# Attention scores from two float32r parts with two heads in the halves of TensorE's array, in place of three 16-bit parts and one head at a time

## What is computed

```python
Q, K, V = proj(Wq, bq), proj(Wk, bk), proj(Wv, bv)
lam = LAMBDA_MAX * jnp.exp(-ALPHA * u_prev)
use_sparse = lam >= SPARSE_THRESHOLD
scores = einsum('bhqd,bhkd->bhqk', Q, K) * scale
dense_out = softmax(scores + lam * where(prior_mask, 0, -1)) @ V
# where use_sparse: attention over 32 listed keys of each query instead
...
x = x + causal_attention(prior_attention(x))
x = x + moe_ffn(gated_mixer(x))
```

## Time and profile before

| | before |
|---|---|
| runs (us) | 1667.03, 1668.97, 1670.23; median 1668.97 |
| span of the profiled execution | 1660.4 us, first to last instruction |
| outside that span, against the median | 8.6 us |
| busy share: TensorE / weight loads / DVE / ACT / POOL | 94% / 46% / 52% / 44% / 42% |
| attention up to 1022.6 us, tail from there | 1022.6 / 637.8 us |

### The profile page before, as it was taken

One profiled execution on the slowest core, in us unless ns is written; L12 is line 12 of the kernel. 1 busy time (PEld: TensorE's weight loads), 2 busy tenths in 40 slices (PEclk: granted clock), 3 DMA queues, 4 the chain that ended last, 5 costly groups with the idle time before them and its releaser, 6 DMA issues. The chain is left out here.

```text
span 1660.4 us, 20515 instructions
## 1 busy us (share of the span) xinstructions
PE 1558.2 (94%) x7392; PEld 762.5 (46%) x7392; DVE 869.0 (52%) x2041; ACT 734.8 (44%) x998; POOL 696.3 (42%) x515
## 2 busy tenths in 40 slices
PE   5789999989999999899999888999999999999998
PEld 3423333323333333333433334555656577777755
DVE  7578878888678855557765733342422111111141
ACT  4754666766566665476645566223211111111111
POOL 4437999987799998143210120400001200000070
PEclk9559999999999999999998898999999999999999
DMA  3551033243231310344532015100040005243071
GB/s 97 143 155 33 24 80 76 70 98 78 60 85 35 79 46 8 79 117 109 125 73 64 28 33 166 61 0 0 0 152 4 22 1 183 92 162 114 16 129 24
DMA packets 75905, 121.43 MB, mean 73 GB/s; under 512 B 14920, under 2 KB 53265, under 8 KB 72731
## 3 DMA queue, kind: packets, MB, share of 16 engines
q1 hardware_dynamic: 72155, 113.62, 24.3%
q0 software_dynamic: 3072, 6.03, 2.1%
q10 hardware_dynamic: 576, 0.47, 0.1%
HBM read 85.08 MB, written 36.96 MB: 74 GB/s over the span
## 5 line engine op out<-in xcount | busy, mean ns | idle before, releaser
L1141 POOL TENSOR_TENSOR sb_prob<-sb_prob,sb_weight 128x1024 f32<-128x1024 f32 x192 | 448.0, 2357 | 44.6 <-ACT sb_prob L1355 44.1
L1355 ACT ACTIVATE sb_prob<-wide 128x1024 f32<-128x1024 f32 (+3 forms) x384 | 347.5, 916 | 207.9 <-PE wide L1965 109.1
L1960 PE MATMUL wide<-sb_stack_q,sb_stack_k 99*128 99x512 bf16 (+3 forms) x896 | 282.8, 364 | 16.2 <-ACT sb_prob L1355 7.4
L1399 ACT ACTIVATE sb_sil<-wide 128x320 f32<-128x320 f32 (+1 forms) x128 | 66.2, 517 | 436.0 <-PE wide L2039 436.0
L1644 DVE CUSTOM_DVE_ANT_0 sb_junk<-bank,sb_bias 128x512 bf16<-128x512 f32 x339 | 226.8, 688 | 61.7 <-PE bank L1933 57.0
L1933 PE MATMUL bank<-sb_stack_k,sb_stack_q 96*128 96x512 bf16 (+3 forms) x597 | 217.3, 380 | 17.1 <-DVE sb_rowmax L1638 5.8
L2039 PE MATMUL wide<-sb_weight,sb_ffn 128*128 128x512 f32 x512 | 232.3, 597 | 0.0
L1980 PE MATMUL wide<-sb_prob,sb_v_aug 128*17 128x512 f32 (+3 forms) x1792 | 221.2, 560 | 7.6 <-ACT sb_o_raw L1368 6.2
L1638 DVE TENSOR_REDUCE sb_rowmax<-bank 128x1 f32<-128x512 f32 (+3 forms) x258 | 139.2, 559 | 88.3 <-PE bank L1936 57.1
L1771 DVE TENSOR_TENSOR sb_act_s<-sb_sil,wide 128x512 f32<-128x512 f32 x64 | 43.9, 687 | 253.3 <-ACT sb_sil L1399 253.3
L1179 POOL DMA_INDIRECT sb_weight<-slots_out,sb_slot_r x32 | 31.5, 984 | 285.0 <-issue 283.2
(11 more groups left out here) (272 smaller groups left out, 1831.7 us busy)
## 6 DMA issues: line engine op xcount, KB each, us to landing
sb_stack_k<-parts SPq DMA_DIRECT2D x32, 256.0 KB, 6.8
o_raw<-sb_o_raw SPq DMA_DIRECT2D x32, 256.0 KB, 2.3
sb_big<-rg SPq DMA_DIRECT2D x8, 1024.0 KB, 4.9
sb_big<-ru SPq DMA_DIRECT2D x8, 1024.0 KB, 7.3
sb_big<-rd SPq DMA_DIRECT2D x8, 1024.0 KB, 10.7
sb_stack_q<-parts SPq DMA_DIRECT2D x16, 384.0 KB, 4.9
parts<-sb_o_norm SPq DMA_DIRECT2D x40, 128.0 KB
sb_stack_q<-parts SPq DMA_DIRECT2D x16, 256.0 KB, 5.4
```

Source lines behind the costliest of these rows:

```text
L1141: e.tensor_tensor(p, p, weight_of(*u[1:]), ALU.mult).then_inc(weigh_p.handle, 1)
L1355: e.activation(p[:, :, first:HALF], sc[:, :, first:HALF], ACT.Exp).then_inc(SC.empty_sem(u), 1)
L1399: e.activation(sil[:, i % 2, 0:n], SC.tile(u)[:, 0:n], ACT.Silu).then_inc(silu_a.handle, 1)
L1960: i = e.matmul(sc[:, j * HALF + first:(j + 1) * HALF], stack_k[0:ROWS_M, n % 3, g, kt * P:(kt + 1) * P], stack_q[0:ROWS_M, n % 3, g, half ...
```

## The change

- Queries and keys are split in two float32r parts (`hi`, rounded by ScalarE, and the rest by one subtraction on POOL), where three 16-bit parts were. `second`, `middle` and `third` become one step, `split`.
- Three products of parts are kept, not six: `ROWS` is 48, with two rows for the maximum 50. Two heads of a pair lie on partitions 0 to 49 and 64 to 113 of one stack; the stack's two rows of -1 come from one memset of the whole `stack_k` by POOL at the start, in place of three DMAs of ones.
- Score matmuls of a unit stand one behind the other, before the `cut` matmuls. Maxima go in pairs of heads, and the diagonal's mask matmuls stand behind both of a pair. The order of the first plan changes with it: two heads' maxima stand with each table.
- `fin` has three steps (VectorE, ScalarE, POOL); `turn` is two steps of four float32r matmuls of 128 columns each, each with four DMAs; the scores of a half wait for its own.
- A stack takes eight DMAs; DRAM parts are float32.

```diff
-PARTS = 3
-Q_PART = [0, 1, 2, 0, 1, 0]
-K_PART = [0, 1, 0, 1, 0, 2]
+PARTS = 2
+Q_PART = [0, 0, 1]
+K_PART = [0, 1, 0]
+STRIP = P // 2
-FIN_STEPS = 6
-FIN_AT = (0, 1, 1, 3, 3, 5, 6, 7)
-STACK_LOADS, LATER = 7, 4
+FIN_STEPS = 3
+FIN_AT = (0, 1, 1, 2, 3, 3)
+STACK_LOADS, LATER = 8, 4
-SPLIT_FIRST, SPLIT_AT = (1, 1, 1), (1, 4, 5)
+SPLIT_WAIT = 1
...
 def maxima(n):
-    return [("max", n, h, qt, half) for h in range(QUAD) for qt in range(NT) for half in range(NH)
-            if not causal or half * HALF < (qt + 1) * P]
+    return [("max", n, h, qt, half) for pair in range(PAIRS_OF) for qt in range(NT) for half in range(NH)
+            for h in range(PAIRS_OF * pair, PAIRS_OF * (pair + 1)) if not causal or half * HALF < (qt + 1) * P]
...
-        return with_tables(maxima(m)) if JOBS[m] == (0, 1, 0) else maxima(m)
+        return in_pairs(with_tables(maxima(m)) if JOBS[m] == (0, 1, 0) else maxima(m))
...
-        plan += [("turn_count", t), ("kb", 0, t)] + [u for u in steps if u[2:4] == (0, t)]
+        plan += [("turn_count", t), ("kb", 0, t)] + [u for u in steps if u[2] < PAIRS_OF and u[3] == t]
...
-    for k, u in enumerate([u for u in steps if u[2]]):
-        plan.append(u)
-        if k % 4 == 0 and tables:
+    for k, pair in enumerate(in_pairs([u for u in steps if u[2] >= PAIRS_OF])):
+        plan += pair
+        if k % 3 != 2 and tables:
             plan += tables.pop(0)
...
-        parts = dram("parts", [2, B, 2, PARTS, DH, H, S], BF16)
+        parts = dram("parts", [2, B, 2, PARTS, DH, H, S], F32)
...
-        stack_q = s1("stack_q", [P, 3, QUAD, S], BF16)
-        stack_k = s1("stack_k", [P, 3, QUAD, S], BF16)
+        stack_q = s1("stack_q", [P, 3, PAIRS_OF, S])
+        stack_k = s1("stack_k", [P, 3, PAIRS_OF, S])
...
+            e.memset(stack_k[:], -1.0).then_inc(const_done.handle, 1)
...
-                if u[0] == "second":
+                if u[0] == "split":
+                    hi, rest = SPLIT[u[1], u[2]][SET[u[1:]]]
                     w.wait_ge(BK.emptied(("product", *u[1:])))
-                    e.tensor_tensor(val, val, hi, ALU.subtract).then_inc(split_p.handle, 1)
-                elif u[0] == "third":
-                    w.wait_ge(split_a.after(("middle", *u[1:])))
-                    e.tensor_tensor(lo, val, mid, ALU.subtract).then_inc(split_p.handle, 1)
+                    e.tensor_tensor(rest.bitcast(F32R), rest, hi, ALU.subtract).then_inc(split_p.handle, 1)
...
-                    i = e.matmul(bk[:, 0:hi - lo], stack_q[0:ROWS, n % 3, h, qt * P:(qt + 1) * P],
-                                 stack_k[0:ROWS, n % 3, h, lo:hi], start=True, stop=not diag)
-                    if diag:
-                        i = e.matmul(bk[:, hi - lo - P:hi - lo], C["ident"], C["neg_qk"], start=False, stop=True)
-                    i.then_inc(BK.full_sem(u), 1)
+                    pair, j = divmod(h, PAIRS_OF)
+                    rows = slice(j * STRIP, j * STRIP + ROWS)
+                    i = e.matmul(bk[:, 0:hi - lo], stack_q[rows, n % 3, pair, qt * P:(qt + 1) * P].bitcast(F32R),
+                                 stack_k[rows, n % 3, pair, lo:hi].bitcast(F32R), start=True, stop=not diag)
+                    if not diag:
+                        i.then_inc(BK.full_sem(u), 1)
+                    elif j == PAIRS_OF - 1:
+                        for g in range(PAIRS_OF):
+                            v = ("max", n, PAIRS_OF * pair + g, qt, half)
+                            e.matmul(BK.tile(v)[:, hi - lo - P:hi - lo], C["ident"], C["neg_qk"], start=False,
+                                     stop=True).then_inc(BK.full_sem(v), 1)
...
                     for j in range(PAIRS_OF):
-                        g = PAIRS_OF * pair + j
+                        rows = slice(j * STRIP, j * STRIP + ROWS_M)
                         i = e.matmul(sc[:, j * HALF + first:(j + 1) * HALF],
-                                     stack_k[0:ROWS_M, n % 3, g, kt * P:(kt + 1) * P],
-                                     stack_q[0:ROWS_M, n % 3, g, half * HALF + first:(half + 1) * HALF],
+                                     stack_k[rows, n % 3, pair, kt * P:(kt + 1) * P].bitcast(F32R),
+                                     stack_q[rows, n % 3, pair, half * HALF + first:(half + 1) * HALF].bitcast(F32R),
                                      start=True, stop=not to_pool(n, v))
-                        if to_pool(n, v):
+                    if to_pool(n, v):
+                        for j in range(PAIRS_OF):
```

205 lines of the change are left out of this document (96 added, 109 removed).

## The result

The changed kernel takes 1793.97 us (median of four runs, 1788.49 to 1807.75) against 1669.6 us for the kernel before: a ratio of 1.0754, 95% interval 1.0727 to 1.0781. It is slower by 7.5%, outside the range given. The profiled execution has a span of 1806.0 us (the run itself 1807.75), 145.6 more than the 1660.4 before. Its mean granted clock was 0.892, that of the other three 0.898 to 0.904, so the excess probably lies where the clock was low; there is one trace only, so this isn't shown.

A forecast was written before the change was run, and what follows sets the result against it. TensorE, busy 94% of the span, was taken as the bound. Prior jobs -30, causal jobs -9 and start -9 made -48 us: 1621 us against the median of 1669, range 1590 to 1680.

The forecast's parts named there:

- I take 0.22: TensorE, scores and maxima: a float32r pair in two row halves takes 0.22 us, between bounds of 0.22 and 0.86.
- Rival 2: TensorE weight loads: a pair's two float32r loads run one after the other, 0.38 us per pair; 1672 us, chance 0.10.
- Rival 3: TensorE pairs: float32r takes two cycles per column or halves don't overlap, 0.43 us per pair; 1712 us, chance 0.14.
- 680 x 0.10 = 68 us: TensorE, prior and causal jobs: 680 added changes between row halves and other arrangements cost 0.10 us each.
- 113 were forecast: Prior jobs, TensorE: scores and maxima in pairs save 512 x 0.22 = 113 us.
- Rival 1, hand-over in pairs: Three banks of maxima: a pair needs two at once, so VectorE and TensorE wait; +22 us, 1643 us, chance 0.14.
- Together -30 of the 77: Prior jobs: of TensorE's net 77 us, 30 shorten the stage, since other engines, mostly POOL, bound it next.
- Causal: of 13 I take -9: Causal jobs: of TensorE's net 13 us saved, 9 shorten the stage, as 38 us are already idle.
- Before the first score: -9: Start: shorter products' chain, filled VectorE waits and a shorter `fin` bring the first score 9 us sooner; bounds -14 and +3.
- the two terms of 4: Start: products' chain without ScalarE's rounding and a POOL subtraction, -4; four maxima filling VectorE's waits, less the hand-over, -4.
- The first score waits for as many DMAs as before: nothing: Start: second `turn` and its DMAs come behind the first half's, so they cost the first score 0 us.
- Small moves at nothing: Larger memset (6.4 us on POOL), identity rounding, 48 more DMA issues (20 us of SP) and doubled stores: all put at nothing.

The follow-up runs named there:

- e8: Changed kernel with both matmuls of each pair (scores and maxima) reading 16-bit constants in place of the float32r stacks: 1725.2 us.
- e4: Kernel before with its 16-bit maxima taken over the first 64 of 96 rows, one head at a time in one row half: 1722.4 us.
- e6: Changed kernel with two heads' rows in one block and every float32r score and maximum matmul over all of them, whole array, nothing side by side: 1748.4 us.
- e9: Changed kernel with each pair of maxima waiting for both banks, and first-batch tables behind every pair of maxima in the first plan: 1825.0 us.
- e1: Changed kernel with the maxima of jobs 1 to 15 one head at a time again, scores still in pairs: 1814.2 us.
- e7: Changed kernel with four extra 16-bit matmuls of 64 rows, two per row half, before each causal pair of scores: 1766.2 us.
- e12: Changed kernel with e7's filler and e9's placing of the tables, without the wait for both banks: 1773.6 us, ratio 1.0627 to the kernel before.
- e10: Changed kernel with e9's two edits and half of e7's filler, one extra matmul in either row half before each causal pair of scores: 1784.0 us.
- e2: Changed kernel with each pair of causal score matmuls issued twice, the second overwriting the first: 1790.3 us.
- e3: Changed kernel with two whole-array 16-bit matmuls of 512 columns ahead of each causal pair of scores, which overwrites them: 1783.7 us.
- e5: Kernel before with its maxima taken over the first 66 of 96 rows: 1666.6 us beside 1670.9 for the kernel before.

## Why the prediction was wrong

**"I take 0.22" for a pair: mis-sized, and not alone to blame.** That halves run at once and float32r takes a column per cycle was right. Measured are 0.34 for a pair behind a change of arrangement or a wait and 0.24 for one that follows a pair directly. The prediction had a price for the change, 0.10, and a price for the pair, and none for a float32r load that lies bare behind the change. In the prior jobs, which have many short runs of pairs, TensorE's records hold some 360 groups of scores or maxima (a pair, or a torn head) that stand behind a change or a wait, and some 260 that follow another directly: 360 x 0.11 + 260 x 0.02 = 45 us. Rival 2 looked at the right thing, the loads, but not at what they do: it had the two of a pair one after the other and 0.38 behind every pair, and the trace has them at once, with 0.24 where nothing is in the way. Its chance was 0.10. Rival 3 is wrong, a pair streams at one column per cycle. And 0.22 would not have saved the forecast: e8 has it, and is 54 us slower than the kernel before. The estimate worked out from the Trainium skill in the prediction ("TensorE: Matmul & The Clock Gate", LDWEIGHTS: two loads make 0.21 and fit under 0.22) comes out for 16-bit operands, whose loads last 0.09 to 0.10 us and whose pairs follow at 0.22 in e8. For float32r the trace doesn't agree: its load lasts 0.18 to 0.19 us, not 0.107.

**"680 x 0.10 = 68 us" of changes: right for the change itself.** Counted in TensorE's records there are 654 and 423 changes in the prior and causal jobs, 256 and 192 before: 629 more (398 prior, where 360 were forecast, and 231 causal, where 330 were). e4 gives 0.09 each, the timeline 0.09 to 0.10.

**The prior jobs in one sum.** I grouped TensorE's records by what follows what, with a pair that starts within 0.045 us as one. "Columns" is what the groups would take at one column per cycle (a float32 pass counted twice), "waits" is the sum of the view of waits, "rest" what is left of the stage:

| prior jobs (us) | columns | waits | rest | stage |
|---|---|---|---|---|
| before | 471.9 | 17.8 | 55.4 | 545.1 |
| e4, changes alone (+597) | 467.4 | 8.0 | 107.4 | 582.9 |
| e6, float32r alone | 468.3 | 20.5 | 99.3 | 588.2 |
| e8, 16-bit pairs (+398 changes) | 395.9 | 67.2 | 98.0 | 561.1 |
| changed (+398 changes) | 388.3 | 49.6 | 149.2 | 587.1 |
| e9, no pair torn | 358.7 | 77.5 | 165.0 | 601.2 |

The columns fell by 84 us where 113 were forecast: the 29 missing are pairs torn in two, and e9, where none is, has them. (44 of the torn maxima start beside a head of the scores in the other half. Counted as one with it, they move 9 us from the columns to the rest, in e8 as in the changed kernel.) Changes of arrangement put 43 us in the rest (e8 against before: 0.11 each), float32r instead of 16-bit operands 51 more (changed against e8), of which 45 are accounted for above. The waits rose by 32. -84 + 43 + 51 + 32 = +42, the stage's loss.

**"Rival 1, hand-over in pairs": right in kind, priced too low, and not the cause alone.** It was 22 us beside a gain. The waits of TensorE grew by 32 and another 29 us of columns were not saved (20, if the 44 above count as side by side). But undoing the pairs (e1) or holding them together (e9) buys nothing: the first gives up the halves, the second waits for VectorE. With three banks both ends cost.

**"Together -30 of the 77": void**. The prediction's own test, prior jobs that don't shrink although the heads run side by side, came out, since TensorE's own work didn't fall: columns and rest together are 10 us more than before. With it went the thought that POOL would be the bound. Its weights' idle time, 44.6 us in the earlier trace rows, doubled:

```profile
L1142 POOL TENSOR_TENSOR sb_prob<-sb_prob,sb_weight 128x1024 f32<-128x1024 f32 x192 | 450.9, 2367 | 88.5 <-ACT sb_prob L1346 87.5
```

**"Causal: of 13 I take -9": the step with the largest error, and in no rival.** It was worked out at the clock that the causal jobs had; the prediction never asked what the clock would be, which puts it at no change. It fell from 0.95 to 0.73, and the jobs lost 98.6 us. At a clock of 0.96 and 0.92 the losses are those of the prior jobs again: e4's changes cost 22 us, e6's float32r 45. How much is the clock? e7 adds 384 pairs of matmuls, 384 x 0.22 = 84 us if none hides in a wait, and its causal jobs still end 34 us sooner than in the changed kernel's slowest run. By medians of four runs each, e12 is 20 us faster than the changed kernel, 4 of them at the start, so the clock costs at least some 16 us even if the filler is free. It may be the whole loss: 456.9 us at 0.73 are 334 us of full clock, and 358.3 at 0.95 are 340. Closer it isn't settled, since what the pairs save at half clock isn't told apart from it. That added work gives time back is shown by e7, e12 and, against e9, e10; e2 and e3 point the same way, within what the changed kernel's own runs lie apart. What brings the clock down is shown only as far as this: scores and maxima in the row halves do, with 16-bit operands (0.81) and with float32r (0.73), and the scores side by side are enough (0.72 in e1); 16-bit maxima in one half, one head at a time, don't (0.96 in e4), nor does whole-array float32r (0.92), and extra matmuls in the whole array or in the halves bring it back (0.95, 0.96). In the windows with 0.53 and 0.54 TensorE's records cover 97% and 95% of the time, so that long idle stretches aren't what went with it. What the chip goes by stays open.

**"Before the first score: -9": forecast and lost.** The last maximum did come sooner, 106.86 instead of 110.87: 4.0 of the 8 us that the two terms of 4 had promised. Then came two things that the prediction put at nothing. The first, in the changed kernel, ScalarE:

```profile
109.39 0.81 ACT L1322 ACTIVATE sb_weight<-sb_y_prior,sb_flags 128x512 f32<-128x512 uint8 x1 [8.01 <-DMA sb_y_prior<-priorT]
110.11 0.70 ACT L1331 ACTIVATE sb_y_prior<-sb_prob,sb_flags 128x512 bf16<-128x512 bf16 x1
110.72 0.70 ACT L1334 ACTIVATE sb_unlisted<-sb_prob,sb_v_aug 128x512 bf16<-128x512 bf16 x1
111.33 0.80 ACT L1322 ACTIVATE sb_weight<-sb_y_prior,sb_flags 128x512 f32<-128x512 uint8 x1
...
113.26 0.24 ACT L1293 ACTIVATE sb_mpart<-sb_top 128x32 fp32r<-128x32 f32 x1
```

The new placing of the tables puts the last two late in the list. ScalarE stands 8.0 us for a load, does both, and only then splits the maxima, 6.4 us after they were known at 106.86; in the kernel before it began 0.25 us after the first of the earlier trace rows, at 111.12. (The load it stands for is issued at 100.93, behind the eight loads of the next stack; such loads are 8.2 us on the way there in the median, 1.8 in the kernel before.) e12 takes the tables out of the way: the maxima are known at 104.42 and ScalarE is there at 104.67. Then the second thing comes up, with its DMAs:

```profile
103.81 0.51 SPq L970 DMA_DIRECT2D sb_stack_k<-parts  x1
...
106.58 5.38 SPq L1018 DMA_DIRECT2D sb_stack_q<-sb_mrow  x8
```

```profile
115.49 0.79 PE L1962 MATMUL wide<-sb_stack_q,sb_stack_k 50*128 50x512 f32 x2 [5.44 <-DMA sb_stack_q<-sb_mrow]
```

The rows of maxima are issued from 106.58 on, behind the eight loads of the next stack, which were issued up to 103.81 and fill the DMA engines:

```profile
100.00:106.00 6.00, 3.99 (x13) 2.08 (x13) 4.54 (x17) 3.08 (x7) 2.59 (x3) 0.50 0.99 250
106.00:115.50 9.50, 4.06 (x14) 2.34 (x11) 0.42 (x1) 2.41 (x4) 0.00 (x0) 0.86 0.98 160
```

They are waited for until 115.49: 6.4 us were gained at the maxima, 3.7 arrive at the first score. "The first score waits for as many DMAs as before: nothing" counted the DMAs and not what lay ahead of them. In the changed kernel itself the DMA engines are idle by then (a share of 0.01 from 113.0 on), and from the first issue of these rows, at 115.50, to the first score are 4.1 us; in e12 they are 8.9. That the loads ahead make the difference is read from these rows and was not tested.

**Small moves at nothing:** nothing here speaks against it; the larger memset takes 5.2 us on POOL, under the 6.4 allowed.

## What to carry to other kernels

Price a matmul by the distance to the next start, and with it ask whether its weight load still fits under its neighbours: behind each change of arrangement the float32r load lay bare, and 0.22 became 0.34 there. Putting work in halves of the array among work on all of it costs 0.10 us at each border, and with float32r 0.11 more behind it, so count borders before savings, and count the banks that the second head needs. Where TensorE's work gets thinner, look at the granted clock as a term of its own; a run with useless matmuls in the stage in question tells in one go whether the clock is part of what is lost.

## What the runs showed of the hardware that was not expected

A float32r matmul of 512 columns is one instruction and streams at one column per cycle: 0.23 us from start to start over the whole array (e6). Its weight load lasts 0.18 to 0.19 us, as a float32 load does, and shows as 0.11 us where it isn't overlapped: behind a change of arrangement or a wait. A pair of float32r matmuls that follows another in the row halves takes 0.24 us, a 16-bit pair 0.22 (e8). Which arrangement a matmul has goes by its rows: 64 rows among whole-array work cost the changes, 66 don't (1722.4 and 1666.6 us, e4 and e5).

More work can take less time: 768 superfluous matmuls, side by side by twos, made the kernel 20 us faster by medians of four runs (e12, 4 of them from the start), and 384 took 41 us off in e10 against e9. And the clock can be at its lower level for nearly all of 110 us (821.2 to 931.3, 0.53 and 0.54) while TensorE's records leave it idle for 3% and 5% only.
